# Local attention layers: query rotary products from PSUM, scaled exponentials, and diagonal blocks laid by DMA

## The reference

```
qkv = x @ Wqkv; 16 heads of 64
q = l2norm(q) * qs;  k = l2norm(k) * ksc
q = q * cos * scale + rotate_half(q) * sin * scale
k = k * cos / scale + rotate_half(k) * sin / scale
sim = q . k * 8, over the window of 32 and the one before it (64 keys a query)
out = softmax(sim) @ v;  x = out @ Wo + x
x = (a * gelu(gate)) @ W2 + b2 + x,   a, gate from layernorm(x) @ W1 + b1
```

## Time and profile before

| | us |
|---|---|
| median of three runs (5169.62 to 5183.22) | 5180.6 |
| the profiled execution | 5172.85 |
| its span in the profile | 5170.8 |
| mean granted clock of PE, as a share of full speed | 0.913 |

### The profile page before, as it was taken

The page is one execution under the profiler, slowest core; times in us unless marked ns, Lnnn a source line. Parts: engine busy times, 40 slices in busy tenths (PEclk is TensorE's granted clock), DMA queues, the critical chain, the costliest instruction groups (busy, mean ns, idle before and its releaser), DMA issues. The chain is left out here.

```text
span 5170.8 us, 110439 instructions
## 1 busy us (share of the span) xinstructions
PE 3934.8 (76%) x39280; PEld 2903.7 (56%) x39280; DVE 4374.4 (85%) x7725; ACT 3040.4 (59%) x4888; POOL 2537.9 (49%) x1612
## 2 busy tenths in 40 slices
PE   5777777777777777767858678777787787777787
PEld 4655655656656646625535466466465565565565
DVE  8988989979979979954335399799799899898897
ACT  4765756746747747722413477477476476575575
POOL 5645646636636636611010266366366365464562
PEclk8988999989989989986978899899899998899899
DMA  1000000000000000021030000000000000000000
GB/s 47 8 23 11 7 22 12 8 27 6 7 27 7 8 25 8 8 62 26 2 74 1 33 7 7 26 8 21 13 8 20 14 8 19 15 7 22 12 7 12
DMA packets 30608, 88.57 MB, mean 17 GB/s; under 512 B 7505, under 2 KB 13649, under 8 KB 28369
## 3 DMA queue, kind: packets, MB, share of 16 engines
q1 hardware_dynamic: 29104, 80.95, 5.9%
q10 hardware_dynamic: 1152, 3.15, 0.2%
HBM read 38.72 MB, written 1.05 MB: 8 GB/s over the span
## 5 line engine op out<-in xcount | busy, mean ns | idle before, releaser
L771 POOL TENSOR_TENSOR pool<-pool 128x512 f32<-128x512 f32 x768 | 1069.1, 1413 | 968.3 <-DVE pool L869 968.3
L776 POOL TENSOR_TENSOR pool<-pool 128x1024 f32<-128x1024 f32 x384 | 1072.8, 2794 | 168.0 <-DVE pool L880 147.2
L443 PE MATMUL psum<-squares,pool 128*128 128x128 f32 x3072 | 475.4, 304 | 420.8 <-POOL pool L776 259.9
L443 PEld LDWEIGHTS psum<-squares,pool 128*128 128x128 f32 x3072 | 368.9, 153 | 587.2 <-issue 338.1
L880 DVE TENSOR_TENSOR pool<-pool 128x1024 f32<-128x1024 f32 x384 | 678.6, 1806 | 6.8
L483 PE MATMUL psum<-wqkv_hi,xs_lo 128*128 128x512 f32 x1152 | 522.2, 453 | 200.3 <-DVE pool L849 104.6
L646 ACT COPY pool<-psum 64x512 f32<-64x512 f32 x768 | 447.1, 582 | 367.1 <-PE psum L443 361.7
L474 PE MATMUL psum<-pool 128*64 128x128 f32 x6144 | 560.7, 296 | 116.7 <-ACT pool L661 116.5
L420 PE MATMUL psum<-pool 128*128 128x128 f32 x3072 | 455.4, 309 | 130.2 <-ACT pool L646 129.8
L859 DVE TENSOR_REDUCE pool<-pool 128x16 f32<-128x1024 f32 x384 | 449.9, 1210 | 88.1 <-ACT pool L685 88.0
L420 PEld LDWEIGHTS psum<-pool 128*128 128x128 f32 x3072 | 420.4, 219 | 179.4 <-ACT pool L646 167.8
(11 more groups left out here) (165 smaller groups left out, 8247.6 us busy)
## 6 DMA issues: line engine op xcount, KB each, us to landing
pool<-pool SPq DMA_DIRECT2D x192, 128.0 KB, 2.3
pool<-in_wqkv SPq DMA_DIRECT2D x12, 1536.0 KB, 6.0
k_st<-turn_st SPq DMA_DIRECT2D x8, 1536.0 KB, 21.3
pool<-in_wo SPq DMA_DIRECT2D x12, 512.0 KB, 3.6
pool<-in_w SPq DMA_DIRECT2D x12, 341.0 KB, 3.0
pool<-in_w SPq DMA_DIRECT2D x12, 192.0 KB, 2.9
rotary<-in_rotary SPq DMA_DIRECT2D x2, 1024.0 KB, 5.4
pool<-in_scale SPq DMA_DIRECT2D x12, 128.0 KB, 6.2
```

The costliest lines, as they stand in the source:

```text
L443: last = pe.transpose(bank(7 - p % 2)[:, P * j:P * j + P], rot[:, p // 2, 2 * c:2 * c + 2, :], ident)
L771: last = g.tensor_tensor(rot[:, q, :, hd * r:hd * r + hd], qn[:, q, :, hd * (1 - r):hd * (2 - r)], tab, ALU.mult)
L776: g.tensor_tensor(rot[:, q], rot[:, q], by_cos[:, q], ALU.add).then_inc(rot_ready, 1)
```

## The change

Four things change in each of the 192 units.

1. Query only: DVE takes `by_cos` and both sine products of q straight from the PSUM banks, unnormalised, at the head of its step (L876 and L879 of the new program), before the sums of squares. `qn` and `by_cos` as before remain for k only. The sine product of q is no longer POOL's.
2. The subtraction of the maximum goes. `raise_top` makes a 128x16 tile `lift` = -maximum x norm; ACT then makes 16 exponentials of 128x64, one a head, straight from the score banks, with the query's norm as scale and `lift` as bias (L679).
3. `diagonal` is no longer eight ACT copies; SP issues eight DMAs of 32 partitions x 16 heads x 32 elements (64 KB in pieces of 128 bytes), one count of `pt_sent` each.
4. Waits follow: the score banks are free when the exponentials are made (`p_ready`) and not when the subtraction is (`s_taken`); `values` waits for the DMAs; the new head of DVE's step waits for unit U's squares of q, for POOL's sum for q of U-1, and for PE's q transposes of U-1.

```diff
+    def diagonal(U):
+        sp.wait_ge(block_ready, done(U))
+        plain(sp)
+        sp.wait_ge(o_ready, done(U - 1))
+        plain(sp)
+        sp.dma_start(pT_last[96:128, :, :], turned_P[0:WIN, :, 0:WIN]).then_inc(pt_sent, 16)
+        for w in range(NW):
+            rows = slice(WIN * w, WIN * w + WIN)
+            if w:
+                sp.dma_start(pT[WIN * (w - 1):WIN * w, :, rows],
+                             turned_P[rows, :, 0:WIN]).then_inc(pt_sent, 16)
+            sp.dma_start(pT[rows, :, rows], turned_P[rows, :, WIN:2 * WIN]).then_inc(pt_sent, 16)
...
+        if has(2):
+            diagonal(U - 2)
...
+    diagonal(U0 + UNITS - 2)
+    diagonal(U0 + UNITS - 1)
...
-            pe.wait_ge(s_taken, done(U - 1))
+            pe.wait_ge(p_ready, done(U - 1))
...
-        pe.wait_ge(pt_ready, done(U))
+        pe.wait_ge(pt_sent, pt_by(U))
...
-            pe.wait_ge(s_taken, done(U - 2))
+            pe.wait_ge(p_ready, done(U - 2))
...
-    def diagonal(U):
-        a.wait_ge(block_ready, done(U))
-        a.wait_ge(o_ready, done(U - 1))
-        a.copy(pT_last[96:128, :, :], turned_P[0:WIN, :, 0:WIN])
-        for w in range(NW):
-            rows = slice(WIN * w, WIN * w + WIN)
-            if w:
-                a.copy(pT[WIN * (w - 1):WIN * w, :, rows], turned_P[rows, :, 0:WIN])
-            last = a.copy(pT[rows, :, rows], turned_P[rows, :, WIN:2 * WIN])
-        last.then_inc(pt_ready, 1)
-    def exponents(U):
-        a.wait_ge(s_taken, done(U))
-        a.activation(S, S, ACT.Exp).then_inc(p_ready, 1)
+    def exponents(U, n):
+        a.wait_ge(top_ready, done(U))
+        a.wait_ge(block_ready, done(U - 1))
+        for h in range(HEADS):
+            last = a.activation(S[:, h, :], bank(4 + h // 8)[:, 2 * WIN * (h % 8):2 * WIN * (h % 8 + 1)],
+                                ACT.Exp, bias=lift[n % 2][:, h:h + 1], scale=norm[n % 4][:, h:h + 1])
+        last.then_inc(p_ready, 1)
...
-        if has(2):
-            diagonal(U0 + 4 * i + k - 2)
...
-            if c == 0 and j == 1:
-                diagonal(last)
...
-            for q in range(2):
-                g.wait_ge(qn_ready, done(U, 2, q))
-                g.wait_ge(t_ready, done(U - 1, 4, 2 * q + 1))
-                plain(g)
-                for r in range(2):
-                    tab = turn[:, bass.ds(t, 1), 2 + q, hd * r:hd * r + hd].broadcast_to(
-                        [P, HEADS, hd])
-                    last = g.tensor_tensor(rot[:, q, :, hd * r:hd * r + hd],
-                                           qn[:, q, :, hd * (1 - r):hd * (2 - r)], tab, ALU.mult)
-                last.then_inc(sin_ready, 1)
-                g.wait_ge(sin_ready, done(U, 2, q))
-                g.wait_ge(cos_ready, done(U, 2, q))
-                g.tensor_tensor(rot[:, q], rot[:, q], by_cos[:, q], ALU.add).then_inc(rot_ready, 1)
+            g.wait_ge(qn_ready, done(U, 2, 0))
+            plain(g)
+            g.tensor_tensor(rot[:, 0], rot[:, 0], by_cos[:, 0], ALU.add).then_inc(rot_ready, 1)
+            g.wait_ge(qn_ready, done(U, 2, 1))
+            g.wait_ge(t_ready, done(U - 1, 4, 3))
+            plain(g)
+            for r in range(2):
+                tab = turn[:, bass.ds(t, 1), 3, hd * r:hd * r + hd].broadcast_to([P, HEADS, hd])
+                last = g.tensor_tensor(rot[:, 1, :, hd * r:hd * r + hd],
+                                       qn[:, 1, :, hd * (1 - r):hd * (2 - r)], tab, ALU.mult)
+            last.then_inc(sin_ready, 1)
+            g.wait_ge(sin_ready, done(U))
+            g.wait_ge(cos_ready, done(U))
+            g.tensor_tensor(rot[:, 1], rot[:, 1], by_cos[:, 1], ALU.add).then_inc(rot_ready, 1)
...
-    def less_top(U):
+    def raise_top(U, n):
         sc = bank(4, 2).rearrange("p (h e) -> p h e", e=2 * WIN)
         v.wait_ge(s_ready, done(U))
         v.tensor_reduce(top, sc, AX.X, ALU.max).then_inc(soft_step, 1)
         v.wait_ge(soft_step, done(U, 5, 0))
-        v.wait_ge(block_ready, done(U - 1))
-        v.tensor_tensor(S, sc, top.unsqueeze(2).broadcast_to([P, HEADS, 2 * WIN]),
-                        ALU.subtract).then_inc(s_taken, 1)
+        v.scalar_tensor_tensor(lift[n % 2], top, -1.0, norm[n % 4][:, 0:HEADS],
+                               ALU.mult, ALU.mult).then_inc(top_ready, 1)
     def step(i, k, has):
         U = U0 + 4 * i + k
         if has(0):
             t = 2 * i + k // 2
+            hd = DH // 2
+            tab = lambda q, part: turn[:, bass.ds(t, 1), q, part].broadcast_to(
+                [P, HEADS, part.stop - part.start])
+            heads = lambda b: bank(b, 2).rearrange("p (h e) -> p h e", e=DH)
+            if k == 0:
+                v.wait_ge(turn_ready, done(l + L0))
+            v.wait_ge(rot_ready, done(U - 1, 2, 0))
+            v.wait_ge(t_ready, done(U - 1, 4, 1))
+            v.wait_ge(sq_ready, done(U, 2, 0))
+            v.tensor_tensor(by_cos[:, 0], heads(0), tab(0, slice(0, DH)), ALU.mult)
+            for r in range(2):
+                to, of = slice(hd * r, hd * r + hd), slice(hd * (1 - r), hd * (2 - r))
+                last = v.tensor_tensor(rot[:, 0, :, to], heads(0)[:, :, of], tab(2, to), ALU.mult)
+            last.then_inc(qn_ready, 1)
             for q in range(2):
                 v.wait_ge(sq_ready, done(U, 2, q))
                 last = v.tensor_reduce(ss[:, HEADS * q:HEADS * (q + 1)],
                                        sq[:, INNER * q:INNER * (q + 1)].rearrange(
                                            "p (h e) -> p h e", e=DH), AX.X, ALU.add)
-            last.then_inc(norm_step, 1)
-            v.wait_ge(norm_step, done(U, RSQRT + 1, 0))
-            rsqrt(v, ss, nwt, norm_step, done(U, RSQRT + 1, 0), ALU.max, 1e-24, None, None,
+            last.then_inc(ss_ready, 1)
+            v.wait_ge(ss_ready, done(U))
+            rsqrt(v, ss, nwt + [norm[k % 4]], norm_step, done(U, RSQRT, -1), ALU.max, 1e-24, None, None,
                   between=probabilities(U - 2) if has(2) else ())
-            v.wait_ge(sin_ready, done(U - 1, 2, 1))
-            v.wait_ge(cos_ready, done(U - 1, 2, 1))
-            for q in range(2):
-                v.tensor_tensor(qn[:, q], bank(2 * q, 2).rearrange("p (h e) -> p h e", e=DH),
-                                nwt[3][:, HEADS * q:HEADS * (q + 1)].unsqueeze(2)
-                                .broadcast_to([P, HEADS, DH]), ALU.mult).then_inc(qn_ready, 1)
+            v.wait_ge(sin_ready, done(U - 1))
+            v.wait_ge(cos_ready, done(U - 1))
+            v.tensor_tensor(qn[:, 1], heads(2), norm[k % 4][:, HEADS:2 * HEADS].unsqueeze(2)
+                            .broadcast_to([P, HEADS, DH]), ALU.mult).then_inc(qn_ready, 1)
             if has(3):
                 residual(U - 3, i, k - 3)
-            if k == 0:
-                v.wait_ge(turn_ready, done(l + L0))
             v.wait_ge(qn_ready, done(U, 2, 1))
             v.wait_ge(rot_ready, done(U - 1, 2, 1))
-            for q in range(2):
-                tab = turn[:, bass.ds(t, 1), q, :].broadcast_to([P, HEADS, DH])
-                v.tensor_tensor(by_cos[:, q], qn[:, q], tab, ALU.mult).then_inc(cos_ready, 1)
+            v.tensor_tensor(by_cos[:, 1], qn[:, 1], tab(1, slice(0, DH)), ALU.mult).then_inc(cos_ready, 1)
         if has(1):
-            less_top(U - 1)
+            raise_top(U - 1, k - 1)
```

More of the change, by code:

```diff
@@ L95, in macaron_program @@
                        rb_ready, w1_ready, w2_ready],
-            "scalar": [xs_ready, sq_ready, v_out, t_out, p_ready, pt_ready, o_out, fsq_ready, gel_ready],
-            "vector": [qn_ready, cos_ready, s_taken, block_ready, y_ready, norm_step, soft_step,
+            "scalar": [xs_ready, sq_ready, v_out, t_out, p_ready, pt_sent, o_out, fsq_ready, gel_ready],
+            "vector": [ss_ready, qn_ready, cos_ready, top_ready, block_ready, y_ready, norm_step, soft_step,
                        xc_ready, diag_ready, xn_ready, hid_ready, x_ready, var_step, aff_step],
@@ L104, in done, with pt_by @@
             return unit * per + part + 1 + CREDIT
+        def pt_by(unit):
+            return (unit + 1) * 16 * 2 * NW + CREDIT
         def mean_bank(c):
@@ L272, in window_half @@
             ss = cut(2 * HEADS)
-            nwt = [cut(2 * HEADS) for _ in range(4)]
+            nwt = [cut(2 * HEADS) for _ in range(3)]
+            norm = [cut(2 * HEADS) for _ in range(4)]
+            lift = [cut(HEADS) for _ in range(2)]
             qT = cut(PAIRS, P)
@@ L311, in tables @@
             def tables(eng, layer):
-                eng.wait_ge(cos_ready, done(layer * UNITS - 1, 2, 1))
-                eng.wait_ge(sin_ready, done(layer * UNITS - 1, 2, 1))
+                eng.wait_ge(cos_ready, done(layer * UNITS - 1))
+                eng.wait_ge(sin_ready, done(layer * UNITS - 1))
                 eng.tensor_tensor(turn.rearrange("p t a e -> p t (a e)"),
@@ L403, in _ @@
                         plain(sp)
-                        sp.wait_ge(sin_ready, done(last, 2, 1))
```

(18 more changed lines are left out.)

6 lines of the change are left out of this document (3 added, 3 removed).

## The result

The changed kernel takes 6306.1 us (median of 4 runs, 6300.9 to 6311.2), the kernel before 5175.7 beside it: ratio 1.218, 95% interval 1.216 to 1.221. The forecast was 5895, its range 5560 to 6310. The time is 411 us above the forecast and inside the range, but only 4 us under its upper end, where the third rival (`lift` loses the port, 6300) put it, with a chance of 0.12.

What follows compares the result with a forecast made beforehand. DVE bounded the kernel (17.96 of 18.11 us a unit); a circle of DVE's step, exponentials and q transposes would make 22.9. 14 units' 67, +3, and -10 give +60 a layer, +720 on 5173: 5895 us, range 5560 to 6310.

Steps and rivals of the forecast that it cites:

- third rival: POOL's sum for k takes the shared port first, `lift` stands 2.4 us, unit 25.3 us, 6300 us in all; chance 0.12.
- DVE's work: DVE's own step in a steady unit, after removals and additions: 15.7 us in place of 18.1.
- What DVE waits for: DVE idles about 7 us a unit before L876, until PE's q transposes of the unit before are done.
- The exponentials: Sixteen 128x64 exponentials on ACT, spaced 0.33 us, 5.3 us a unit in place of 1.06.
- `lift` wins the port: At the end of DVE's step `lift`, ready at 2.26 us, precedes POOL's sum for k, near 2.35; margin 0.1.
- Circle 2: DVE's step to the 32x32 transposes, eight DMAs, values, v product, q transposes: 22.1 us a unit, 0.8 under circle 1.
- circle 1: DVE's whole step 15.7, exponentials 5.3, then ACT and PE to the q transposes 2.2: 23.2, taken as 22.9 us.
- The end part: End of each layer, Newton chain and gelus less delayed: net -10 us a layer, bounds -20 to +10.
- The small form: Rival: per-partition pointers cost nothing, exponentials 0.14 to 0.2 us each, Circle 2 decides at 21.3, 5630 us; chance 0.17.
- faster: Case: the wait for the q transposes never bites, a unit takes 15.7 us, 4650 us in all; chance 0.03.
- The pieces decide: Rival: DMAs of 128-byte pieces cost 0.93 us an issue, Circle 2 is 24.7 us, 6195 in all; chance 0.16.
- The signs: Expected in the profile after: DVE idle before L876, PE idle before `values` or the v product, L145's 1.7 us stall gone.

Runs made afterwards that it cites:

- experiment 1: The changed kernel with POOL's sum for k made to wait for `lift`, so `lift` cannot lose the port: 6266.9 us, ratio 1.211.
- Experiment 5: The changed kernel with two buffers for the rotated q, so DVE's head waits for q transposes of two units before: 5316.6 us, ratio 1.0265.
- experiment 8: The changed kernel with `lift` first, plus six unread matmuls on PE before the wait for the diagonal blocks and the `y_ready` wait moved ahead: 6014.8 us, ratio 1.164.
- experiment 7: The changed kernel with `lift` first and only four of the eight DMAs of a unit, one `rot`: 5906.5 us, ratio 1.140.

## Why the prediction was right or wrong

- **DVE's work** (15.7): right. 17.42 busy less 2.15 of `lift`'s standing is 15.3, and in experiment 1 the exponentials start 15.6 us behind the first product from PSUM in the mean. L149 no longer stands, L898 takes 2.14 for 2.0.
- **What DVE waits for**: right, in place and size: 7.2 us before L876, ended by PE's transposes; 7 were named. Experiment 5 shows it is that buffer.
- **The exponentials**: 4.85 for 5.3; they stand 0.29 apart, for 0.33. **From their end to L876**: 2.34 for 2.2 in the unit shown.
- **`lift` wins the port** (in the forecast's 22.9): this step failed. I let L898 need 1.0 after it gets the port; the maximum behind it starts 1.13 later (271.07 less 269.94, the start of L782 plus one half of 1.3), and the margin was 0.1. POOL's sum is where I had it, 2.34 behind that moment for 2.35; `lift` comes at 2.39 for 2.26. So POOL's sum came first, by 0.05 us in the unit shown, and `lift` stood in 180 of 192 units. The rival's 25.3 was measured as 24.85 to 25.05.
- **Circle 2** (22.1): failed by two terms; it is 24.8. Eight issues stand 0.68 apart, 0.08 more than taken, and from the last transpose to the first value it is 7.6 for 6.7. I priced the values at 2.9 from a stretch in which PE had been idle for 0.63 only and had its full clock, though the change itself makes PE wait 3.3 to 3.7 just before them. They take 4.8. I named a lower clock and called it covered by the bounds, but put no number on it. It was 1.5 us a unit, 252 us (experiment 8).
- **The two together**: with `lift` put right alone, the time is still within 1% of the measured one (experiment 1). The other single correction was not run alone, but circle 1 with `lift` standing is 24.85 by itself. The rival of 6300 therefore named what the trace shows and the right time, but the wrong price of the race: not 400 us (6300 - 5895) but 39, since a second circle is just as long. That one number fits is partly luck: the range reached to 6310 for this rival, and the time would have been 6267 without it. With `lift` first and circle 2 shortened (experiment 7) the time is 5906.
- **The end part** (-10 a layer, +3 for the second unit): -0.8 there and -2.4 in the first spacing, so -3.2 a layer for the -7 forecast, with the sign of the +3 wrong. The chain's standing beside POOL's weight conversion did move: into the second chunk of the feed-forward part, where L153 takes 2.19 and L156 4.36. The gain of 10 in the end part was mis-sized, not its sign.
- **The small form** and **faster** are refuted by 0.29 an exponential. **The pieces decide** is refuted at 0.68 an issue, under its 0.93; yet the circle it spoke of is the one that decides once `lift` is first. Its 0.93 was worked out from no row.
- **The signs**: PE idles before the values, DVE before L876, and L149 no longer stands, as named. A unit above 24.5 was to refute my price of an exponential or of a DMA. It came (25.05), and neither price was the main error: it was the race and the clock of the values.
- **Slips without weight**: 5893 and the 8 us of the median make 5901, not 5895. In the profile before, the attention in the middle is the 18th to 23rd of 40 slices, and DVE is at 7 to 9 tenths elsewhere, not 8 or 9.

## What to carry to other kernels

When a change lengthens a chain that closes through a buffer, count every circle through that buffer and compare their lengths: removing one stall gives only the distance to the next circle (39 us here), and one more copy of the buffer opened all of them (990 us). Price PE's work behind a new wait at the clock it gets after waiting, not at that of the busy stretch it was measured in. When two instructions come to a shared port within an instruction's scatter, fix their order with a wait, or take the worse case as the forecast. Of what was tried, the changed kernel with two buffers and `lift` first is 0.9% faster than the kernel before, and the DMAs alone 0.65%.

## What the runs showed of the hardware

- A DMA of 64 KB from SBUF to SBUF in 512 pieces of 128 bytes took 0.64 us to issue and landed in 2.4 us; one of 128 KB in 32 pieces landed in 2.3. The issue took 0.08 to 0.13 longer than that of the larger one (0.507 before, 0.56 in the changed kernel), and the landing about the same.
- Sixteen exponentials of 128x64 with a per-partition scale and bias, back to back on ACT, take 4.85 us: 0.29 apart, though each takes 0.44.
- Extra matmuls on an idle PE made the kernel 252 us faster, with its other instructions unchanged but for one wait moved ahead: the values ran at a granted clock of 0.93 in the mean in place of 0.58.
